# Convolution results of a step leave in one transfer of 128 partitions, into a buffer laid out by channel group

## The reference

```python
x = x + conv(_ln_c(x))            # _ln_c: normalised over the 64 channels of each pixel
t = tokens(x)                     # 50176 tokens of 64 values
t = t + moe(_ln_t(t))             # 8 experts, hidden 256, the best two of each token
# conv, for a map v:
r   = relu(batchnorm(w1 @ v + b1))            # 64 -> 16 channels
ker = w2 @ r + b2                             # 49 x 16 groups: a 7 x 7 filter for every pixel and group
out[b, g, d, y, x] = sum over i, j of pad(v)[b, g, d, y + i, x + j] * ker[b, g, 7 * i + j, y, x]
```

## Time and profile before

| what | us |
|---|---|
| median of three runs | 2610.99 |
| lowest and highest | 2604.84, 2629.76 |
| the profiled execution | 2621.96 |
| its span | 2619.3 |
| first and last copy into `ob` (steps 0 and 63) | 222.7 and 1438.5 |

### The profile page before, as it was taken

One profiled execution on the slowest core, in us unless ns is written; L12 is line 12 of the kernel. 1 busy time (PEld: TensorE's weight loads), 2 busy tenths in 40 slices (PEclk: granted clock), 3 DMA queues, 4 the chain that ended last, 5 costly groups with the idle time before them and its releaser, 6 DMA issues. The chain is left out here.

```text
span 2619.3 us, 34529 instructions
## 1 busy us (share of the span) xinstructions
PE 2025.6 (77%) x10208; PEld 1223.9 (47%) x10208; DVE 1506.3 (58%) x2687; ACT 829.4 (32%) x1540; POOL 961.0 (37%) x1011
## 2 busy tenths in 40 slices
PE   8959889898898998899898321477778777787855
PEld 5735444454444455445454321345455445454534
DVE  4536666566778777786787535245444444444434
ACT  3421111122222222222222211355445454554520
POOL 6110000004242142331343566155555555555540
PEclk9969999999899999899999555689898898988976
DMA  9877777778776777777773311666667666676539
GB/s 278 176 149 193 184 178 186 196 196 195 181 198 171 203 196 194 182 193 183 195 207 90 89 55 46 174 192 194 187 200 196 194 187 196 195 195 190 164 104 356
DMA packets 284717, 474.16 MB, mean 181 GB/s; under 512 B 116144, under 2 KB 188387, under 8 KB 261565
## 3 DMA queue, kind: packets, MB, share of 16 engines
q1 hardware_dynamic: 247965, 423.23, 60.5%
q0 software_dynamic: 30528, 34.27, 4.8%
q10 hardware_dynamic: 6048, 14.57, 1.5%
HBM read 392.67 MB, written 81.93 MB: 181 GB/s over the span
## 5 line engine op out<-in xcount | busy, mean ns | idle before, releaser
L967 POOL DMA_INDIRECT token_rows<-gate_rows,gate_index x392 | 408.3, 1042 | 1043.4 <-DVE gate_index L1289 930.8
L1167 DVE TENSOR_TENSOR prod<-z_ps,r_all 119x896 f32<-119x896 f32 x512 | 544.8, 1084 | 221.5 <-PE z_ps L1080 110.2
L1500 POOL DMA_INDIRECT mixed<-exp_mix,exp_xt x474 | 491.0, 1036 | 409.8 <-DVE exp_mix L1639 282.7
L1523 ACT ACTIVATE exp_hid<-exp_h_ps,exp_pack 128x384 f32<-128x384 f32 x632 | 349.1, 575 | 419.3 <-PE exp_h_ps L1567 192.8
L1084 PE MATMUL z_ps<-xq,band 112*119 112x448 f32 x1024 | 440.2, 565 | 44.3 <-DVE prod L1167 38.4
L1567 PE MATMUL exp_h_ps<-exp_tok,exp_pack 128*128 128x384 f32 x1264 | 293.0, 377 | 61.7 <-issue 61.2
L1084 PEld LDWEIGHTS z_ps<-xq,band 112*119 112x119 f32 x1024 | 182.1, 187 | 254.8 <-issue 190.7
L1567 PEld LDWEIGHTS exp_h_ps<-exp_tok,exp_pack 128*128 128x128 f32 x1264 | 237.1, 208 | 79.9 <-issue 74.2
L1097 PE MATMUL o_ps<-prod,pick 119*32 119x448 f32 x2048 | 247.9, 578 | 26.9 <-issue 17.2
L1579 PE MATMUL exp_y_ps<-exp_hid,exp_pack 128*64 128x384 f32 x1264 | 262.4, 540 | 1.1 <-issue 1.1
L1078 PE MATMUL z_ps<-xq_hi,band_hi 119*119 119x448 f32 x512 | 215.1, 420 | 51.3 <-DVE xq_lo L1156 21.7
(11 more groups left out here) (205 smaller groups left out, 2161.6 us busy)
## 6 DMA issues: line engine op xcount, KB each, us to landing
xq<-xs SPq DMA_DIRECT2D x192, 896.0 KB
exp_pack<-packs SPq DMA_DIRECT2D x316, 321.5 KB
exp_xt<-token_rows SPq DMA_DIRECT2D x158, 120.0 KB
xs<-xpad SPq DMA_DIRECT2D x32, 448.0 KB, 5.8
xin<-in_x_dram SPq DMA_DIRECT2D x8, 1568.0 KB, 11.0
co<-ob SPq DMA_DIRECT2D x512, 24.5 KB
merge_yt<-mixed ACTq DMA_DIRECT2D x28, 448.0 KB, 6.0
mixed<-exp_mix,exp_xt POOLq DMA_INDIRECT x474
```

The source lines that it names most:

```text
L967: pool.indirect_dma_start(out=token_rows[:, :], out_offset=bass.IndirectOffsetOnAxis(ap=index[b % RR][:, j:j + 1], axis=0), in_=rows[b % R ...
L1167: nc.vector.tensor_tensor(prod[(NU * t + u) % PR][:, :, :].rearrange("p m (d x) -> p m d x", d=D), z_ps[(NU * t + u) % 3][0:MF, :, 0:CN].r ...
L1500: pool.indirect_dma_start(out=mixed[:, :], out_offset=bass.IndirectOffsetOnAxis(ap=xt[t % XT][:, j, ROW_ID:ROW_ID + 1].bitcast(U32), axis= ...
L1523: nc.scalar.activation(hid[n % 8][:, :], h_ps[n % HT][:, 0:N], ACT.Gelu, bias=pack[t % WT][:, e, PACK_B1 + blk:PACK_B1 + blk + 1]).then_in ...
```

## The change

The buffer `co` gets another shape. It was images x channels x rows x columns. It becomes half x parity x group x image of the pair (i) x channel of the group (d) x pair (q) x 32 rows x 56 columns, so the four rows of padding that the sums' 128 partitions hold go to memory too. A step's result then leaves in one transfer of 128 partitions with eight runs of 56 floats each (1024 runs) in place of eight transfers of 28 partitions with four such runs each (896 runs). ACT writes `ob` with image and channel exchanged. Both readers of `co` address it through a new function; the runs that they read stay as long as they were. Semaphore counts follow.

```diff
-    co = nc.dram_tensor("co", (B, C, H, W), F32)
+    co = nc.dram_tensor("co", (2, PARITY, G, 2, D, CH, 32 * W), F32)
...
+def conv_run(co, img, at, size):
+
+    s, pos = divmod(at, HALF)
+    return co[s, img % PARITY, :, img // PARITY % 2, :, img // (2 * PARITY), pos:pos + size]
...
                 sp.wait_ge(ob_done, t + 1)
-                for q in range(CH):
-                    for i in range(2):
-                        dst = co[2 * (2 * q + i) + par, D * g:D * (g + 1), HALF_ROWS * s:HALF_ROWS * (s + 1), :]
-                        sp.dma_start(dst.rearrange("d h w -> h d w"),
-                                     ob[t % 2][32 * q:32 * q + HALF_ROWS, :]
-                                     .rearrange("p (d i w) -> p d i w", d=D, i=2)[:, :, i, :]).then_inc(ob_out[t % 2], 16)
+                dst = co[s, par, g].rearrange("i d q (h w) -> (q h) (i d) w", w=W)
+                sp.dma_start(dst, ob[t % 2][:, :].rearrange("p (e w) -> p e w", w=W)).then_inc(ob_out[t % 2], 16)
...
-                    for lot, part in enumerate((x, co)):
-                        sp.dma_start(xc[n % XC][C * lot:C * (lot + 1), to:to + size],
-                                     part[img].rearrange("c h w -> c (h w)")[:, at:at + size]
-                                     ).then_inc(xc_in[n % XC], 16)
+                    sp.dma_start(xc[n % XC][0:C, to:to + size],
+                                 x[img].rearrange("c h w -> c (h w)")[:, at:at + size]).then_inc(xc_in[n % XC], 16)
+                    sp.dma_start(xc[n % XC][C:2 * C, to:to + size],
+                                 conv_run(co, img, at, size)).then_inc(xc_in[n % XC], 16)
...
-                nc.scalar.activation(ob[t % 2][:, :], o_ps[:, 0:CN], ACT.Copy).then_inc(ob_done, 1)
+                nc.scalar.activation(ob[t % 2][:, :].rearrange("p (i d w) -> p d i w", i=2, d=D),
+                                     o_ps[:, 0:CN].rearrange("p (d i w) -> p d i w", d=D, i=2),
+                                     ACT.Copy).then_inc(ob_done, 1)
...
                         sp.dma_start(conv[d % CT][lanes, to:to + size],
-                                     co[img].rearrange("c h w -> c (h w)")[:, at:at + size]
-                                     ).then_inc(conv_in[d % CT], 16)
+                                     conv_run(co, img, at, size)).then_inc(conv_in[d % CT], 16)
```

More of the change, by code:

```diff
@@ L910, in load_chunk @@
                     for i in range(2):
-                        sp.wait_ge(ob_out[i], (n // QUARTER_CHUNKS + 1) * G // 2 * 2 * CH * 16)
+                        sp.wait_ge(ob_out[i], (n // QUARTER_CHUNKS + 1) * G // 2 * 16)
                 if n >= XC:
@@ L997, in evacuate @@
                 act.wait_ge(summed, t + 1)
-                act.wait_ge(ob_out[t % 2], t // 2 * 2 * CH * 16)
-                nc.scalar.activation(ob[t % 2][:, :], o_ps[:, 0:CN], ACT.Copy).then_inc(ob_done, 1)
+                act.wait_ge(ob_out[t % 2], t // 2 * 16)
+                nc.scalar.activation(ob[t % 2][:, :].rearrange("p (i d w) -> p d i w", i=2, d=D),
+                                     o_ps[:, 0:CN].rearrange("p (d i w) -> p d i w", d=D, i=2),
+                                     ACT.Copy).then_inc(ob_done, 1)
             def take_unit(n):
```

## The result

The changed kernel takes 2596.32 us (median of 20 runs, 2574.98 to 2609.39); the kernel before took 2611.91 in the same series (20 runs, 2600.32 to 2630.05). The ratio is 0.9926, 95% interval 0.9905 to 0.9947, so a gain of some 19 us (14 to 25). One of experiment 1's six runs (2604.62 us) is left out of its ratio as a slow one; with it the means give 0.993. The two profiled executions are 19.1 us apart (2621.96 and 2602.85), though each lies above its median. The range of 2582 to 2630 us holds the result, and "within 1%" holds too; but the gain is five times the 4 us that the sum gave, and that has to be explained.

A forecast was written before the change was run, and what follows sets the result against it. The prediction took one DMA engine carrying the whole filter band to bound the first quarter and about 40 of 63 intervals. Its terms, -4 us for completion packets and 0 elsewhere, gave 2607 us, range 2582 to 2630.

The forecast's parts named there:

- within 1%: Whole kernel: the time stays between 2585 and 2637 us, given a chance of 0.74.
- The bound: Convolution stage: one DMA engine carries the whole filter band, the other fifteen wait some 4 us, setting the first quarter's pace.
- The 40 intervals of the sum: Convolution steps: the engine carrying the band sets about 40 of 63 intervals, at 0.10 us saved a step.
- the loads of `co` at 0: Reading back `co`: loads keep count and size, the later one has 0.0 idle before its addition; 0 us.
- One sign that the prediction gave for being wrong towards faster: Convolution steps: copies into `ob` closer together than 19.3 us; PE's wait for the chunk gone was named beside it.
- The term of -4 us: Store on the band's engine: seven of eight completion packets a step go, 15 ns each, over 40 intervals.
- SP's time: 0: SP's queue: 2.8 us a step freed at the stores gains 0, covered by the band engine's backlog.
- the first rival: SP's queue makes loads late, so freeing it gains: 39 us (2572), or 128 us (2483) at most; chance 0.15.
- eight commands fewer: SP's queue: that many fewer commands stand between the store's wait and the chunk loads and next band behind it.
- The merging rule: Store transfers: merge small ones, about 2.0 us fixed cost each; seven a step would make 896 us, which the prediction doubted.
- The hold-up rival: Store: one large transfer delays the chunk and band queued behind it; +16 us (2627) or +227 us (2838); chance 0.12.
- PE with DVE the rest: Later convolution rounds: PE and DVE set the intervals that the band's engine does not, out of 63.

The follow-up runs named there:

- experiment 1: Changed kernel with each step's store issued again as eight commands of 16 partitions, new layout kept; 2582.95 us, ratio 0.9902.
- experiment 4: Kernel before (eight stores, old layout) with the filter band loaded in two commands, 112 rows over 16 engines and 7 rows; 2502.27 us, ratio 0.9599.
- experiment 3: Changed kernel with the filter band loaded in two commands, 112 rows over 16 engines and the last 7 rows; 2474.43 us, ratio 0.9498.
- 10: Changed kernel with eight store commands in the new layout and the filter band split in two commands; 2433.63 us, ratio 0.9495.
- 8: Changed kernel with the band split in two commands and each step's store issued by ACT instead of SP; 2475.13 us, ratio 0.9482.
- experiment 5: Changed kernel with the old eight commands (28 rows by 4 channels, 14 engines), new addresses and `ob` order kept; 2591.13 us, ratio 0.9946.
- 6: Kernel before with only the order in `ob` changed, two images one behind the other; 2602.53 us, ratio 1.0002.
- 7: Kernel before with 64 rows per channel of `co` in place of 56, the last 8 empty; 2602.76 us, ratio 0.9981.
- 11: Kernel before with GpSimd's 14 scatters meant to run in two lots of 7 by an added wait; 2569.33 us, ratio 1.0009.
- 12: Changed kernel with the band split in two commands and the scatters meant to run in two lots of 7; 2433.92 us, ratio 0.9493.
- experiment 2: Changed kernel with 50 already met semaphore waits behind SP's store of each step; 2613.29 us, ratio 1.0064.

## Why the prediction was right, and where it was not

*The bound.* Right: one engine carries the band alone and sets the pace of the first quarter; splitting the band takes some 39 us from that quarter alone (276.9 to 238.1 in experiment 4). The 40 intervals of the sum are not shown: no run counts them, and the split also takes 64 us from the later 47 (915.6 to 852.1).

*The step that failed* is that the sum costs the store by runs, bytes and engines, and the loads of `co` at 0 because they "keep count and size". Where the runs lie in memory had no term at all. The addresses by group measured -0.54% with the old commands (-14 us); the whole new layout measured -0.7 to -1.1%, with the full engine (the changed kernel, experiment 1) or without it (3 and 10 against 4). So that the time fell into the range is luck as far as the cause goes: the range was wide enough for a gain that no term of the sum stands for. One sign that the prediction gave for being wrong towards faster did come: the copies into `ob` are 19.0 us apart on the mean, before 19.3.

*The term of -4 us* for completion packets isn't confirmed. Packets of 4 B on SP's queue went from 27,031 to 20,887 in the whole program (6144 fewer, which is 512 commands on 14 engines less 64 on 16), but eight commands (0.9902) are no slower than one (0.9926). It is below what these runs can tell.

*SP's time: 0.* Right, and more widely than I argued: the backlog of the full engine covers it in the first quarter, and without that cover it still counts for nothing that can be told (experiments 8 and 10). So the first rival named the right sign for a wrong reason; after the change PE waits longer for the chunk than before (36.5 against 29.2). (The prediction's "eight commands fewer" are seven.)

*The merging rule* of the Trainium skill (DMA: Bandwidth & Descriptors, "Rules for kernel authors") weighed in the prediction has the runs against it here: experiment 1 puts seven transfers a step back and loses nothing. The 2.0 us that the prediction takes with it stand in the Trainium skill (the same page, "Anatomy of one DMA") for GpSimd's path, whereas SP issues these stores.

*The hold-up rival* didn't come: the store's packets on the other engines ran from 386 to 389, ahead of the band engine's at 391.70.

*The later rounds.* "PE with DVE the rest" was too coarse. In them a stall of VectorE and PE of 2 to 6 us, and the half clock after it, makes the band late. There are fewer in the profile after than before, but not in experiment 5 against 6, so they aren't shown to carry the gain. What follows the gain, between kernels of one chip, is the stretch from the store to the next band: 1.9 us in experiment 5 against 2.3 and 2.1 in 6 and 7, and 4.0 in experiment 3 against 5.5 in 4. How addresses come to do that is **open**: both the stores and the loads of `co` have new ones (the load of a chunk is also written as 16 groups by 4 channels), and no run parted them. That the gain appears only where `co` is read back speaks for the reads or for reads and writes together, but weakly: in the first quarter the band engine sets the pace, and PE with the band split, and either would hide a gain of the store. The loads' packets don't decide it: those of 3584 B (from x and `co`, 505 to 1600) took 215.7 ns on the mean before and 212.1 after, but also 211.8 in experiment 5 and 211.0 in 6. Whether the stall's late release is the memory's, or the same that made SP's met waits slow, isn't shown either.

## What to carry to other kernels

Cost a change of layout by its addresses too, or widen the range for what can't be costed; and before believing that fewer commands gain, put the commands back into the new layout. A DMA share of 0.75 with stretches at 0.06 is an invitation: give the one loaded transfer an outermost dimension that spreads over all engines, which here gained 5%, some seven times the change. A delay made of many small instructions has to be measured in its own trace before its result is read, and so has a wait that is to split a burst: in experiments 11 and 12 it split nothing. And compare a profile's run with its kernel's median before two profiles are subtracted.

## What the runs showed of the hardware

In experiment 2 SP's waits on semaphores that are already met take some 0.03 us each outside of GpSimd's scatter bursts (1057 recorded, median 28 ns). Within the bursts 125 of 463 recorded ones took over 0.4 us, mostly some 0.7, and nearly all the rest were as short as outside; transfers that SP issues in a burst aren't slowed alike (0.64 us for the store at 923.03).

PE's granted clock was 1.00 at 784 to 786, when PE had just stopped, and 0.50 at 788 to 790, when it worked again, so such a stall is paid for twice; in experiment 3 PE never pauses from 300 to 440, and the clock is 1.00 throughout.
